# Where the query norms are applied in a local attention: from the vectors to the scale of the exponentials

## The chip, the cores and the metric

The kernel runs on one core of a Trainium2 chip. The metric is device time in microseconds (us) of one execution, as the median of several. A core has a matrix engine (PE), a vector engine (DVE), an activation engine (ACT), a general engine (POOL) and DMA queues. They run side by side and meet only at semaphores. SBUF is the memory that all of them use, PSUM the one that PE writes. "Granted clock" is the share of PE's full speed that the chip allowed in a stretch.

## The reference

Two layers, each an attention and a feed-forward block, on 8 x 128 tokens of width 128. The change touches only the last block, a local transformer of depth 2. Its attention, cut to what matters (8 heads of 64, window 64, 8 tiles of 128 tokens per depth):

```python
q = l2norm(q) * qs
k = l2norm(k) * ksc
q, k = rotary_xpos(q, k)
bq = q.reshape(b, h, w, WINDOW, d) * QK_SCALE
sim = jnp.einsum('bhwid,bhwjd->bhwij', bq, bk)
sim = jnp.where(mask, -jnp.finfo(sim.dtype).max, sim)
attn = jax.nn.softmax(sim, axis=-1)
out = jnp.einsum('bhwij,bhwjd->bhwid', attn, bv)
```

`l2norm(t)` divides each head's vector by its length. A row of `sim` belongs to one query, so the inverse length of that query is one factor for the whole row.

## The kernel before, in words

The program is written by hand, one instruction list for each engine, with counting semaphores between them. Nothing reorders it. On DVE and ACT a `step(...)` marks an instruction as counted, and `settle()` waits until all counted instructions of the own engine have ended.

The local attention takes 2 x 8 = 16 **local tiles** i = 0 to 15 (128 tokens, all 8 heads). For tile i:

- PE `qkv(i)` projects queries and keys (1024 columns) and values (512) into PSUM banks 0 to 2. ACT `square(i)` (L1493) squares queries and keys and signals `squared`.
- DVE `rotate(i)` (L1190, L1192, L1194) waits for `squared`, multiplies by the rotary tables into R and T2; POOL adds T2 to R (L1724). DVE `sum_squares(i)` gives 16 sums per token (8 query heads, 8 key heads), ACT `head_root(i)` a first inverse root.
- DVE `unit_norm(i)` refines the 16 inverse lengths in three small steps (`newton`, L875, L877, L879) into `lr` and multiplies all 1024 columns of R by them (L1209). It signals `rope`.
- PE `turn_qk(i)` (L582) turns R, ACT `take_turned_qk(i)` (L1516, L1517) copies the result out. PE `score_band(i)` writes the band mask (`BANDED` outside the window) and `score_heads(i)` adds the scores (both L252) in banks 3 and 4.
- DVE `largest(i)` (L1216) takes the negated maximum of every row and head into `lneg` and signals `lmax`.
- ACT `exponential_half(i, c)` (L1525) has one ACTIVATE for each of 4 heads: `exp(score + bias)`, bias a column of `lneg`, and an accumulator read for the row sum. It signals `lexp`. Both halves are 8 ACTIVATEs of 128x128.
- DVE `normalise_p(i, c)` (L1229, L1232) divides by the sums, PE `turn_p`, ACT `take_turned_p` (L1538), PE `weigh`, ACT `take_turned_o` (L1510), PE `project_o`, DVE `add_output` (L1224) finish the tile.

The tiles are pipelined: while tile i is in its exponentials, tile i+1 is normalised and tile i+2 projected and rotated. In tiles 0 to 3 ACT runs `exponential(i)`, then `square(i+2)`. From tile 4 on, the feed-forward block goes along in quarters and tiles alternate:

- an **even tile** has the first half of its exponentials, then `square(i+2)`, then the second half, then the copy L1555 (Identity with a scale and a bias from SBUF), later `take_gelu` (L1565);
- an **odd tile** has all eight exponentials, and only then `square(i+2)`.

DVE's order in an even tile from 4 on is: `largest(i)`, `unit_norm(i+1)`, `quarter_rows`, `rotate(i+2)`, `sum_squares(i+2)`, `add_output(i-1)`, both `normalise_p(i)`, three `gate_third`. In an odd tile: `largest(i)`, `unit_norm(i+1)`, both `normalise_p(i)`, `add_down` (L1252), `rotate(i+2)`, moments, `sum_squares(i+2)`, `add_output(i-1)`.

Of the kernel before, what the change touches and what calls it, by code (L numbers as in the profile page):

```python
# [18 lines left out]
ALU = mybir.AluOpType  # L19
ACT = mybir.ActivationFunctionType  # L20
AX = mybir.AxisListType

P = 128
# [4 lines left out]
LH, LD = 8, 64  # L28
# [7 lines left out]
HD = 6  # L36
EPS = 1e-5
MASKED = -float(2 ** 66)
BANDED = -float(2 ** 100)
QMAX = 127.0  # L40
SOFT = 1.0 / float(np.sqrt(np.float32(D)))

# [28 lines left out]
def constants():  # L71
# [4 lines left out]
    i, j = np.arange(P)[:, None], np.arange(P)[None]  # L76
    c[:, C_BAND:C_BAND + P] = np.where((i < j) | (i > j + 64), BANDED, 0.0)
    c[:, C_ROWMASK:C_ROWMASK + HG] = (np.arange(P)[:, None] % 64) // D == np.arange(HG)[None]
# [14 lines left out]
def build(nc, x_d, ctxT_d, maskT_d, const_d, l0_d, ffn0_d, l1_d, f_d, out_d):  # L93
    with ExitStack() as stack:
        def sb(name, shape, dt=F32):
            return stack.enter_context(nc.sbuf_tensor(name, [P, *shape], dt))
# [3 lines left out]
        def sem(name):  # L100
            if name not in sems:
                sems[name] = stack.enter_context(nc.semaphore(name))
            return sems[name]
# [67 lines left out]
        lneg = sb("lneg", [2, LH])  # L171
        tabs = sb("tabs", [2, 2, 2, LD])
        ss = sb("ss", [2 * LH])
        ss_floor = sb("ss_floor", [2 * LH, 2])
        lss = sb("lss", [2 * LH])
        lr0 = sb("lr0", [2 * LH])
        lnt = sb("lnt", [2, 2 * LH])
        lr = sb("lr", [2 * LH])
        lsum = sb("lsum", [2, LH])
        lrec = sb("lrec", [LH])  # L180

# [1 line left out]
        def view(base, at, *shape):  # L183
            size = int(np.prod(shape))
            names = "abcd"[:len(shape)]
            v = base[:, at:at + size]
            return v if len(shape) == 1 else v.rearrange(f"p ({' '.join(names)}) -> p {' '.join(names)}",
                                                         **dict(zip(names, shape)))
# [3 lines left out]
        ps = stack.enter_context(nc.psum_tensor("ps", [P, 8, 512], F32))  # L192
# [20 lines left out]
        R = view(blkf, 0, 2, T)  # L213
# [619 lines left out]
        def _(dve):  # L833
            v = nc.vector
            done = [0]

            def step(i):

                i.then_inc(sem("dve_steps"), 1)
                done[0] += 1  # L840

            def settle():

                dve.wait_ge(sem("dve_steps"), done[0])
# [28 lines left out]
            def newton(x, r, tmp, out):  # L873

                step(v.tensor_tensor(tmp[:, 0, :], r, r, ALU.mult))  # L875
                settle()
                step(v.scalar_tensor_tensor(tmp[:, 1, :], tmp[:, 0, :], -0.5, x, ALU.mult, ALU.mult))  # L877
                settle()
                step(v.scalar_tensor_tensor(out, tmp[:, 1, :], 1.5, r, ALU.add, ALU.mult))  # L879
                settle()  # L880
# [229 lines left out]
            for u in range(6):  # L1110
                c, t, r = u // 3, u % 3, FT0[u % 3]
                h = HID0[0:r, t, 512 * c:512 * (c + 1)]
# [91 lines left out]
            def unit_norm(i):  # L1204
                dve.wait_ge(sem("root"), i + 1)
                dve.wait_ge(sem("pair_sum"), i + 1)
                newton(ss[:, :], lr0[:, :], lnt, lr[:, :])
                r = R[:, i % 2, :].rearrange("p (h j) -> p h j", j=LD)
                v.tensor_tensor(r, r, lr[:, :].rearrange("p (h o) -> p h o", o=1).to_broadcast([P, 2 * LH, LD]),  # L1209
                                ALU.mult).then_inc(sem("rope"), 1)  # L1210

            def largest(i):
                dve.wait_ge(sem("lscores"), i + 1)
                if i >= 2:
                    dve.wait_ge(sem("lexp"), 2 * (i - 1))
                v.tensor_reduce(lneg[:, i % 2, :], ps[:, 3:5, :].rearrange("p b (h k) -> p (b h) k", k=P),  # L1216
                                AX.X, ALU.max, negate=True).then_inc(sem("lmax"), 1)

            def add_output(i):
                n = i % NB  # L1220
# [42 lines left out]
            sum_squares(0)  # L1263
            divide_batch(4)
            unit_norm(0)
            divide_batch(5)
            rotate(1)
            sum_squares(1)
            largest(0)
            divide_batch(6)  # L1270
            unit_norm(1)
            for i in range(4):
                if i >= 1:
                    largest(i)
                if i == 0:
                    divide_batch(7)
                if i >= 1:
                    unit_norm(i + 1)
                if i == 1:
                    normalise(6, X, Z, "z_in", 4, NB)  # L1280
                normalise_p(i, 0)
                normalise_p(i, 1)
                rotate(i + 2)
                sum_squares(i + 2)
                if i == 0:
                    add_projection(1, 1)
                    moments(6, X, 4, NB)
                if i >= 1:
                    add_output(i - 1)
                if i == 3:  # L1290
                    quarter_moments(0)
            for i in range(4, 2 * NB, 2):
                largest(i)
                unit_norm(i + 1)
                quarter_rows((i - 4) // 2)
                if i + 2 < 2 * NB:
                    rotate(i + 2)
                    sum_squares(i + 2)
                add_output(i - 1)
                normalise_p(i, 0)  # L1300
                normalise_p(i, 1)
                if i + 2 == 2 * NB:
                    break

                i, q = i + 1, (i - 4) // 2
                for t in range(3):
                    gate_third(q, t)
                largest(i)
                unit_norm(i + 1)
                normalise_p(i, 0)  # L1310
                normalise_p(i, 1)
                add_down(q)
                rotate(i + 2)
                quarter_moments(q + 1)
                sum_squares(i + 2)
                add_output(i - 1)
# [18 lines left out]
        def _(act):  # L1335
# [3 lines left out]
            def step(i):  # L1339
                i.then_inc(sem("act_steps"), 1)  # L1340
                done[0] += 1

            def settle():
                act.wait_ge(sem("act_steps"), done[0])
# [30 lines left out]
            def take_output(k, c):  # L1375
# [15 lines left out]
              bias=w_x[:, A_BQK + 2:A_BQK + 3]).then_inc(sem("proj"), 1)  # L1391
# [3 lines left out]
              bias=w_x[:, A_BQK:A_BQK + 1]).then_inc(sem("proj"), 1)  # L1395
# [22 lines left out]
            for i in range(G * NCH + 2):  # L1418
# [10 lines left out]
                if i >= 2:  # L1429
                    c, q = i - 2, (i - 2) % NCH * QC  # L1430
# [24 lines left out]
            for u in range(6):  # L1455
                t, r = u % 3, FT0[u % 3]
# [62 lines left out]
            def exponential_half(i, c):  # L1519
                act.wait_ge(sem("lmax"), i + 1)  # L1520
                if i >= 2:
                    act.wait_ge(sem("pT_ps"), 2 * (i - 1))
                for j in range(4):
                    k = 4 * c + j
                    e = a(S1[:, i % 2, P * k:P * (k + 1)], ps[:, 3 + c, P * j:P * (j + 1)], ACT.Exp,  # L1525
                          bias=lneg[:, i % 2, k:k + 1], accum_out=lsum[:, i % 2, k:k + 1])
                e.then_inc(sem("lexp"), 1)

            def exponential(i):
                exponential_half(i, 0)  # L1530
                exponential_half(i, 1)
# [94 lines left out]
            for i in range(4, 2 * NB, 2):  # L1626
                q, more = (i - 4) // 2, i + 2 < 2 * NB
                take_turned_o(i - 1)
                exponential_half(i, 0)
                if more:  # L1630
                    square(i + 2)
# [13 lines left out]
                i = i + 1  # L1645
# [130 lines left out]
```

## Time and profile before

| | us |
|---|---|
| median of 3 runs | 408.64 |
| lowest, highest | 405.45, 411.32 |
| span of the profiled execution, first to last instruction | 406.5 |
| busy: PE, DVE, ACT, POOL | 352.7, 338.9, 295.9, 58.6 |

The profile has no other time of the profiled execution than its span. The span stands against the median only roughly: it lies 2.1 us below it and inside the spread of the runs. The local tiles fill the stretch from about 205 us to 388 us. Busy time says how long an engine worked, not whether somebody waited for it.

### The profile page before, as it was taken

The numbers are of one execution on the slowest core, as the hardware profiler recorded it, in microseconds if no ns is written. First come the engines' busy times: TensorE is split into PE (matmuls) and PEld (weight loads), VectorE is DVE, ScalarE is ACT, GpSimd is POOL, SyncE is SP. The second block draws the span as 40 slices with busy tenths as digits, with TensorE's granted clock in tenths as the row PEclk, the third lists the DMA queues.
The fourth block names the chain that finished last, engine by engine and source line by source line (L and its number), as shares of the span: only waits on it lengthen the run. The fifth ranks groups of instructions, "written<-read, shape, count | busy, mean of one in ns | idle before, by whom it ended". The sixth has DMA issues, their size and how long they took to land.

```text
span 406.5 us, 10233 instructions
## 1 busy us (share of the span) xinstructions
PE 352.7 (87%) x4033; PEld 251.1 (62%) x4036; DVE 338.9 (83%) x725; ACT 295.9 (73%) x727; POOL 58.6 (14%) x45
## 2 busy tenths in 40 slices
PE   2899999999945878998798889999999999998676
PEld 1498888887731424555455556567676767676565
DVE  5989987887789889979679999989899999986343
ACT  1789999896434337776747787898989898986663
POOL 2000002000003021000023123403132323212110
PEclk9999999999985699999989999999999999999779
DMA  8800010000000000000000000000000000000001
GB/s 315 347 4 3 4 42 3 3 4 3 2 0 0 2 1 0 2 2 2 0 2 2 0 0 2 0 2 2 1 2 2 1 2 0 2 2 0 2 1 52
DMA packets 1774, 8.29 MB, mean 20 GB/s; under 512 B 192, under 2 KB 448, under 8 KB 1472
## 3 DMA queue, kind: packets, MB, share of 16 engines
q1 hardware_dynamic: 1728, 7.65, 4.8%
q8 instruction: 32, 0.52, 0.6%
q14 instruction: 14, 0.11, 0.1%
HBM read 7.12 MB, written 0.52 MB: 19 GB/s over the span
## 4 chain that ended last, share of the span: by engine, by line
PE 43%; DVE 29%; ACT 17%; issue 10%; DMA 1%; DVEq 0%; ACTq 0%
PE ps L252 15%; ACT PT L1525 5%; ACT blk L1411 3%; DVE PT L1232 3%; PE ps L506 3%; DVE lneg L1216 3%; PE ps L620 3%; DVE blk L1190 2%; DVE ss_floor L1200 2%; PE ps L656 2%; ACT PT L1595 2%; PE ps L379 2%; PE ps L493 2%; DVE Y L870 2%; PE ps L582 2%
## 5 line engine op out<-in xcount | busy, mean ns | idle before, releaser
L1724 POOL TENSOR_TENSOR blk<-blk 128x1024 f32<-128x1024 f32 x16 | 37.7, 2359 | 170.6 <-DVE blk L1194 170.6
L568 PE MATMUL ps<-w_f,full 128*128 128x512 f32 x96 | 48.2, 619 | 0.9 <-issue 0.9
L1525 ACT ACTIVATE PT<-ps,lneg 128x128 f32<-128x128 f32 x128 | 45.0, 377 | 5.3 <-DVE lneg L1216 5.3
L252 PEld LDWEIGHTS ps<-blk,st 128*128 128x128 bf16 x768 | 26.8, 98 | 3.8
L1045 DVE TENSOR_REDUCE mneg<-ps 128x4 bf16<-128x512 bf16 x32 | 22.0, 688 | 7.7 <-PE ps L357 7.4
L1525 ACT ACTIVATION_READ_ACCUMULATOR PT<-ps,lneg 128x1 f32 x128 | 27.9, 218 | 0.0
L252 PE MATMUL ps<-blk,rel 128*128 128x64 bf16 x768 | 27.6, 193 | 0.0
L252 PE MATMUL ps<-blk,st 128*128 128x64 bf16 x768 | 27.6, 193 | 0.0
L1582 ACT ACTIVATE PT<-ps 128x512 f32<-128x512 f32 x32 | 17.5, 595 | 13.2 <-PE ps L506 13.2
L1216 DVE TENSOR_REDUCE lneg<-ps 128x8 f32<-128x1024 f32 x16 | 19.6, 1223 | 8.6 <-PE ps L252 8.5
L1232 DVE TENSOR_TENSOR PT<-PT,lrec 128x512 f32<-128x512 f32 x32 | 25.3, 790 | 1.1
L568 PEld LDWEIGHTS ps<-w_f,full 128*128 128x128 f32 x96 | 16.3, 192 | 13.7 <-issue 13.6
L252 PEld LDWEIGHTS ps<-blk,rel 128*128 128x128 bf16 x768 | 24.6, 98 | 0.0
L1426 ACT ACTIVATE St<-ps 128x512 bf16<-128x512 f32 x32 | 19.3, 604 | 7.0 <-PE ps L252 6.9
L620 PE MATMUL ps<-const,PT 128*128 128x128 f32 x128 | 19.3, 288 | 5.5 <-ACT blk L1517 2.9
L506 PEld LDWEIGHTS ps<-const,PT 128*128 128x128 f32 x128 | 14.1, 143 | 15.1 <-ACT PT L1595 13.8
L1411 ACT ACTIVATE blk<-blk,const 128x128 bf16<-128x128 bf16 x32 | 23.3, 984 | 0.0
L656 PE MATMUL ps<-YT,w_f 128*128 128x256 f32 (+1 forms) x96 | 22.5, 384 | 0.6 <-DVE blk L1194 0.3
L1190 DVE TENSOR_TENSOR blk<-ps,tabs 128x1024 f32<-128x1024 f32 x16 | 19.5, 1218 | 3.8 <-ACT blk L1493 3.8
L1538 ACT ACTIVATE PT<-ps 128x512 f32<-128x512 f32 x32 | 17.5, 602 | 5.6 <-PE ps L620 5.6
L620 PEld LDWEIGHTS ps<-const,PT 128*128 128x128 f32 x128 | 14.5, 145 | 10.3 <-ACT blk L1517 3.7
L506 PE MATMUL ps<-const,PT 128*128 128x128 f32 x128 | 17.9, 284 | 3.1 <-ACT PT L1595 2.8
(234 smaller groups left out, 905.5 us busy)
## 6 DMA issues: line engine op xcount, KB each, us to landing
w_f<-f_dram SPq DMA_DIRECT2D x2, 1689.0 KB, 13.3
w_x<-l_dram SPq DMA_DIRECT2D x1, 774.0 KB, 5.9
w_f<-ffn_dram SPq DMA_DIRECT2D x1, 561.0 KB, 7.9
X<-x_dram SPq DMA_DIRECT2D x1, 512.0 KB, 3.6
ctxT<-ctxT_dram SPq DMA_DIRECT2D x1, 512.0 KB, 4.4
OT<-maskT_dram SPq DMA_DIRECT2D x1, 512.0 KB, 7.1
rest<-l_dram SPq DMA_DIRECT2D x1, 385.0 KB, 4.8
const<-const_dram SPq DMA_DIRECT2D x1, 324.0 KB, 6.3
```

What stands on the lines that cost most here:

```text
L252: return mm(out, l, r, start=start, stop=False, skip_group_check=True)
L506: i = tr(ps[:, 4 + c, P * j:P * (j + 1)], S1[:, u % 2, P * (4 * c + j):P * (4 * c + j + 1)], ident)
L568: m = mm(ps[:, c, :], hT[:, n, :], w_f[:, l, F_QKV + 512 * c:F_QKV + 512 * (c + 1)], start=True, stop=True)
L620: t = tr(ps[:, 5 + c, P * j:P * (j + 1)], S1[:, i % 2, P * (4 * c + j):P * (4 * c + j + 1)], ident)
L656: x = mm(ps[0:r, first + t, 256 * m:256 * (m + 1)], w_f[:, l, F_W1 + HID * m + P * t:F_W1 + HID * m + P * t + r], YT[:, 256 * j:256 * (j + ...
L1045: v.tensor_reduce(mneg[:, c % 2, :], turned_b[:, c % 2, :].rearrange("p (j k) -> p j k", j=4), AX.X, ALU.max).then_inc(sem("chunk_max"), 1)
L1190: step(v.tensor_tensor(heads(R[:, i % 2, :]), u, tab[:, 0].to_broadcast([P, 2, LH, LD]), ALU.mult))
L1216: v.tensor_reduce(lneg[:, i % 2, :], ps[:, 3:5, :].rearrange("p b (h k) -> p (b h) k", k=P), AX.X, ALU.max, negate=True).then_inc(sem("lma ...
L1232: v.tensor_tensor(p, p, r.rearrange("p (h o) -> p h o", o=1).to_broadcast([P, 4, P]), ALU.mult)\
L1411: i = a(ring[:, c % RING, :, :, :, h].rearrange("p b n q -> p (b n) q"), src, ACT.Copy, scale=const[:, C_ROWMASK + h:C_ROWMASK + h + 1])
L1525: e = a(S1[:, i % 2, P * k:P * (k + 1)], ps[:, 3 + c, P * j:P * (j + 1)], ACT.Exp, bias=lneg[:, i % 2, k:k + 1], accum_out=lsum[:, i % 2, ...
L1724: g_.tensor_tensor(R[:, i % 2, :], R[:, i % 2, :], T2, ALU.add).then_inc(sem("pair_sum"), 1)
```

## The change

The queries stay unnormalised. Their inverse lengths come in later: once in the maximum (`lbias` = `lneg` times the inverse length, a small new instruction on DVE behind the maximum), and once as the per-token scale of the exponential, which becomes `exp(scale * score + bias)` with both operands from SBUF. L1209 covers the 512 columns of the keys alone. `lr` gets two buffers, since it is now read by ACT later on. `BANDED` is smaller, so that its product with an inverse length stays finite.

```diff
-BANDED = -float(2 ** 100)
+BANDED = -float(2 ** 80)
...
-        lr = sb("lr", [2 * LH])
+        lr = sb("lr", [2, 2 * LH])
+        lbias = sb("lbias", [2, LH])
...
-                newton(ss[:, :], lr0[:, :], lnt, lr[:, :])
-                r = R[:, i % 2, :].rearrange("p (h j) -> p h j", j=LD)
-                v.tensor_tensor(r, r, lr[:, :].rearrange("p (h o) -> p h o", o=1).to_broadcast([P, 2 * LH, LD]),
+                rate = lr[:, i % 2, :]
+                newton(ss[:, :], lr0[:, :], lnt, rate)
+                r = R[:, i % 2, 512:1024].rearrange("p (h j) -> p h j", j=LD)
+                v.tensor_tensor(r, r, rate[:, LH:2 * LH].rearrange("p (h o) -> p h o", o=1).to_broadcast([P, LH, LD]),
                                 ALU.mult).then_inc(sem("rope"), 1)
...
-                v.tensor_reduce(lneg[:, i % 2, :], ps[:, 3:5, :].rearrange("p b (h k) -> p (b h) k", k=P),
-                                AX.X, ALU.max, negate=True).then_inc(sem("lmax"), 1)
+                step(v.tensor_reduce(lneg[:, i % 2, :], ps[:, 3:5, :].rearrange("p b (h k) -> p (b h) k", k=P),
+                                     AX.X, ALU.max, negate=True))
+                settle()
+                v.tensor_tensor(lbias[:, i % 2, :].rearrange("p (c j) -> p c j", c=2),
+                                lneg[:, i % 2, :].rearrange("p (c j) -> p c j", c=2),
+                                lr[:, i % 2, 0:LH].rearrange("p (j c) -> p c j", c=2), ALU.mult).then_inc(sem("lmax"), 1)
...
                     e = a(S1[:, i % 2, P * k:P * (k + 1)], ps[:, 3 + c, P * j:P * (j + 1)], ACT.Exp,
-                          bias=lneg[:, i % 2, k:k + 1], accum_out=lsum[:, i % 2, k:k + 1])
+                          scale=lr[:, i % 2, 2 * j + c:2 * j + c + 1], bias=lbias[:, i % 2, k:k + 1], accum_out=lsum[:, i % 2, k:k + 1])
```

DVE in an even tile i from 4 on, from the maximum of tile i to the rotation of tile i+2, as it was:

```order
L1216 TENSOR_REDUCE lneg<-ps 128x8
L875 TENSOR_TENSOR lnt<-lr 128x16
L877 SCALAR_TENSOR_TENSOR lnt<-lnt,ss 128x16
L879 SCALAR_TENSOR_TENSOR lr<-lnt,lr 128x16
L1209 TENSOR_TENSOR blk<-blk,lr 128x1024
L875 TENSOR_TENSOR nt<-r 128x2
L877 SCALAR_TENSOR_TENSOR nt<-nt,ve 128x2
L879 SCALAR_TENSOR_TENSOR rstd<-nt,r 128x2
L870 TENSOR_SCALAR Y<-O,mv,rstd 128x128 x2
L1190 TENSOR_TENSOR blk<-ps,tabs 128x1024
```

And as it is now (`blk` is R, line numbers are 1 to 6 higher):

```order
L1218 TENSOR_REDUCE lneg<-ps 128x8
L1221 TENSOR_TENSOR lbias<-lneg,lr 128x8
L876 TENSOR_TENSOR lnt<-lr 128x16
L878 SCALAR_TENSOR_TENSOR lnt<-lnt,ss 128x16
L880 SCALAR_TENSOR_TENSOR lr<-lnt,lr 128x16
L1211 TENSOR_TENSOR blk<-blk,lr 128x512
L876 TENSOR_TENSOR nt<-r 128x2
L878 SCALAR_TENSOR_TENSOR nt<-nt,ve 128x2
L880 SCALAR_TENSOR_TENSOR rstd<-nt,r 128x2
L871 TENSOR_SCALAR Y<-O,mv,rstd 128x128 x2
L1191 TENSOR_TENSOR blk<-ps,tabs 128x1024
```

One instruction is added between the maximum and its signal, and the multiplication is half as wide. On ACT nothing changes place; the exponentials of the same even tile and what follows them now read:

```order
L1516 ACTIVATE full<-ps 128x512
L1531 ACTIVATE PT,lsum<-ps,lbias,lr 128x128 x4
L1499 ACTIVATE blk<-ps 128x1024
L1531 ACTIVATE PT,lsum<-ps,lbias,lr 128x128 x4
L1561 ACTIVATE YT<-ps,w_f 128x256
```

Each of the 8 exponentials of a tile names two SBUF operands (`lbias`, `lr`) where it named one (`lneg`).

## Rows read from the trace of the kernel before

**Rows 1.** The page: span, and busy time of each engine.
```profile
span 406.5 us, 10233 instructions
...
PE 352.7 (87%) x4033; PEld 251.1 (62%) x4036; DVE 338.9 (83%) x725; ACT 295.9 (73%) x727; POOL 58.6 (14%) x45
```

**Rows 2.** Chain of waits (start us, us, what) in odd tile 7.
```profile
292.51 1.18 ACT PT L1525 x6
```

**Rows 3.** Timeline of DVE (start us, us), tiles 7 and 8.
```profile
293.72 0.18 DVE L1229 RECIPROCAL lrec<-lsum 128x4 f32<-128x4 f32 x1 [0.40 <-ACT PT L1525]
...
299.86 1.22 DVE L1216 TENSOR_REDUCE lneg<-ps 128x8 f32<-128x1024 f32 x1 [0.16 <-PE ps L252]
301.00 0.17 DVE L875 TENSOR_TENSOR lnt<-lr 128x16 f32<-128x16 f32 x1
301.20 0.17 DVE L877 SCALAR_TENSOR_TENSOR lnt<-lnt,ss 128x16 f32<-128x16 f32 x1
...
301.62 1.23 DVE L1209 TENSOR_TENSOR blk<-blk,lr 128x1024 f32<-128x1024 f32 x1
...
303.87 1.22 DVE L1190 TENSOR_TENSOR blk<-ps,tabs 128x1024 f32<-128x1024 f32 x1
...
309.38 0.69 DVE L1232 TENSOR_TENSOR PT<-PT,lrec 128x512 f32<-128x512 f32 x1
```

**Rows 4.** Timeline of ACT, the same two tiles.
```profile
290.79 0.37 ACT L1525 ACTIVATE PT<-ps,lneg 128x128 f32<-128x128 f32 x1 [0.30 <-DVE lneg L1216]
...
293.54 1.06 ACT L1493 ACTIVATE blk<-ps 128x1024 f32<-128x1024 f32 x1
...
300.89 0.60 ACT L1510 ACTIVATE full<-ps 128x512 f32<-128x512 f32 x1 [0.80 <-PE ps L628]
301.38 0.36 ACT L1525 ACTIVATE PT<-ps,lneg 128x128 f32<-128x128 f32 x1
...
301.72 0.37 ACT L1525 ACTIVATE PT<-ps,lneg 128x128 f32<-128x128 f32 x1
...
302.79 1.02 ACT L1493 ACTIVATE blk<-ps 128x1024 f32<-128x1024 f32 x1
...
305.08 0.59 ACT L1555 ACTIVATE YT<-ps,w_f 128x256 f32<-128x256 f32 x1
305.53 0.62 ACT L1499 ACTIVATE blk<-ps 128x512 f32<-128x512 f32 x1
...
309.43 1.19 ACT L1565 ACTIVATE PT<-ps,w_f 128x256 f32<-128x256 f32 x3
```

**Rows 5.** Groups by line and shape, ACT, whole span (busy us, mean ns).
```profile
L1538 ACT ACTIVATE PT<-ps 128x512 f32<-128x512 f32 x32 | 17.5, 602 | 5.6 <-PE ps L620 5.6
...
L1565 ACT ACTIVATE PT<-ps,w_f 128x256 f32<-128x256 f32 x16 | 6.8, 470 | 0.6 <-PE ps L656 0.4
...
L1555 ACT ACTIVATE YT<-ps,w_f 128x256 f32<-128x256 f32 x8 | 4.6, 581 | 1.3 <-PE ps L649 1.3
...
L1460 ACT ACTIVATE PT<-ps,gusc 128x512 f32<-128x512 f32 x4 | 2.7, 687 | 2.7 <-PE ps L454 2.6
```

**Rows 6.** Timelines of ACT and DVE: squares and rotations behind tiles 0 and 1.
```profile
218.89 1.07 ACT L1493 ACTIVATE blk<-ps 128x1024 f32<-128x1024 f32 x1
...
230.19 1.06 ACT L1493 ACTIVATE blk<-ps 128x1024 f32<-128x1024 f32 x1
...
220.40 1.22 DVE L1190 TENSOR_TENSOR blk<-ps,tabs 128x1024 f32<-128x1024 f32 x1
...
232.32 1.22 DVE L1190 TENSOR_TENSOR blk<-ps,tabs 128x1024 f32<-128x1024 f32 x1
```

**Rows 7.** Windows: us, busy us (instructions) of each engine, granted clock, DMA.
```profile
289.50:299.90 10.40, 10.19 (x82) 7.73 (x84) 9.54 (x22) 9.50 (x32) 2.53 (x2) 1.00 0.01 2
...
366.90:377.40 10.50, 8.51 (x74) 7.10 (x76) 5.77 (x15) 6.38 (x24) 1.33 (x3) 1.00 0.00 0
...
382.10:388.40 6.30, 5.34 (x32) 4.30 (x30) 2.94 (x13) 2.39 (x7) 1.57 (x2) 0.55 0.02 4
```

## The prediction

> **What bounds the kernel now.** I read the page's busy times first, then windows of one tile each, then the chain of waits through two tiles, and last the timelines of DVE and ACT beside each other. By busy time PE and DVE lead and ACT trails [rows 1], which would favour a change that takes work off DVE. The window of an odd tile says less: in 10.40 us PE is busy 10.19, DVE 9.54, ACT 9.50 [rows 7]. All three are nearly full, so what counts is who waits last, and that differs between even and odd tiles.
>
> In an **odd tile** the chain runs through ACT: maximum, all eight exponentials [rows 2], then the second row sums, for which DVE sat idle 0.40 us [rows 3], then DVE and PE to the scores of the next tile. The square for the rotation also stands behind the eight exponentials [rows 4]. Whatever DVE saves between the maximum and those row sums only lengthens its idle time.
>
> In an **even tile** the chain is shown on DVE: maximum, newton, L1209, the rows of the feed-forward, rotation. But the rotation starts at 303.87 [rows 3] and needs the square, which ends at 302.79 + 1.02 = 303.81 [rows 4]. Between the two lie 0.06 us, of which I count 0.03 as slack and 0.03 as the release. So ACT is a second chain of the same length: the copy L1510 at 300.89, four exponentials from 301.38, the square at 302.79. Behind the rotation DVE is in one piece up to the row sums, and PE waits for it.
>
> **The change part by part.**
>
> *L1209 at half width.* 128x1024 takes 1.23 us; 128x512 of the same operation with the same kinds of operands takes 0.69 (L1232) [rows 3]. Saved: 0.54 us of DVE in each of 16 tiles.
>
> *The new `lbias`.* An instruction of this size is L875 with 0.17 us, and one that waits for it starts 0.20 after its start [rows 3]. It must wait for the end of the maximum: 1.22 us and 0.03 to release, where L875 now starts 1.14 behind the maximum's start [rows 3]. So DVE loses 0.11 for the wait and some 0.10 for the instruction, whose end overlaps L875: 0.21 us. DVE's net is -0.33 us a tile. The signal `lmax` comes 0.20 us later. Queued behind the wait is newton for the next tile, which nobody needs at once; waiting for `lmax` is ACT. In odd tiles ACT was idle 0.30 us at that point [rows 4], so it starts 0.20 later. In even tiles ACT is held by L1510: the first exponential starts at 301.38, and the later `lmax` comes at 299.86 + 1.22 + 0.03 + 0.20 = 301.31, which costs nothing.
>
> *The second operand from SBUF.* This is the term that decides, and no row shows such an exponential. With no such operand a 128x512 activation takes 602 ns, with a scale from SBUF (L1460) 687: +85. A 128x256 one with a bias takes 470 (L1565), with scale and bias 581 (L1555): +111 [rows 5]. From start to start, which is what a queue pays, L1565 needs (1.19 - 0.47) / 2 = 0.36 us and L1555 305.53 - 305.08 = 0.45 [rows 4]: +0.09. These rows bound it at 0.085 and 0.111; below them stands nothing at all, if the accumulator read behind each exponential hides it. I take 0.09, because L1555 also stands in the queue directly behind an exponential's accumulator read. The pitch of an exponential is 301.72 - 301.38 = 0.34 [rows 4] and becomes 0.43: +0.72 us for eight, +0.36 for four. The Trainium skill ("ScalarE: Activation LUTs", section "What ACT_TABLE_LOAD costs") speaks against the change in the same way: it gives about 93 ns for each per-partition pointer operand. By it the eight would cost 0.74; no run here shows it for an exponential with accumulator.
>
> *Wider effects.* `lr`'s second buffer and `BANDED` cost nothing: no instruction changes shape. POOL, PE and the DMA queues issue the same instructions in the same order. `rope` comes earlier, but PE turns tile i+1 only behind work that waits for the exponentials.
>
> *Odd tiles.* DVE's 0.33 us fall into its idle time before the second row sums. The chain grows by 0.20 + 0.72 = 0.92 us. The square ends 0.92 later too, with the row sums and the rotation. Tiles 5, 7, 9, 11, 13, 15: 5.5 us. In tile 15 the end of the kernel hangs on the same eight exponentials.
>
> *Even tiles.* The square ends 0.36 later, 0.03 of it is slack: the rotation starts 0.33 us later, although DVE would be ready 0.33 earlier. Six tiles, 4 to 14 (14 has no rotation, but the copy L1555 behind its exponentials feeds PE; I give it the same): 2.0 us. The second half's 0.36 goes into the row sums four microseconds later and is hidden by the rotation; if that cover went, it would cost 0.36 more a tile.
>
> *Tiles 0 to 3* have all exponentials ahead of the square. Tile 0: the square ends at 218.89 + 1.07 = 219.96, DVE rotates at 220.40 [rows 6], so 0.44 - 0.03 of 0.92 are covered: +0.51. Tile 1: the square ends at 230.19 + 1.06 = 231.25, moved by 0.51 + 0.92 to 232.68, the rotation from 232.32 [rows 6] to 232.71: the running sum falls from 0.51 to 0.39. Tiles 2 and 3 have the idle time of odd tiles: +0.92 each. Together 2.2 us.
>
> **Sum:** 2.2 + 2.0 + 5.5 = +9.7 us, or 406.5 [rows 1] to 416.2 of the profiled execution. Its span is 2.1 us below the median of the runs; on 408.64 the forecast is 418.3, +2.4%. With 0.085 and 0.111 in place of 0.09 the some 104 exponentials on the path (ten tiles with eight, six with four) give -0.5 and +2.2: +9.2 to +11.9.
>
> **The rivals.**
>
> *The second operand is free* (15%). For it speaks that the accumulator read could cover a fetch; against it, that an accumulator read also precedes L1555, and L1555 pays. Then odd tiles pay 0.20 for `lmax` (six, and two of the first four), even tiles gain 0.03, tiles 0 and 1 gain 0.2 to 0.3 each: 1.6 - 0.2 - 0.5 = +0.9 us, 409.5. Same within 2%.
>
> *DVE is the bound after all* (5%), as the chain shows it in even tiles. Then every tile gains 0.33: 16 x 0.33 = 5.3 us, 403.3, not slower. It needs a free second operand and a square that ends 0.33 us before DVE comes, where the rows leave 0.06; it decides from the point where the four exponentials get shorter, not longer. The Trainium skill ("VectorE: DVE Perf Modes", section "The DRAIN you can't avoid") says that the next DVE operation starts only when the pipe is empty and that a semaphore between two costs nothing extra. By it `settle()` would be free and the gain 16 x 0.44 = 7.0 us, 401.6. The trace disagrees: L875 starts 0.08 us before the maximum ends [rows 3].
>
> *PE's clock falls* (8%). PE gets longer pauses, and in the window 382.10 to 388.40, which follows tile 15's pauses, the clock is 0.55 [rows 7]. If it fell like that for half of PE's 10.19 us in an odd tile [rows 7], that half would take twice as long, 5.1 us more; in five tiles 25 us, 444. Against it: PE was busy 8.51 of 10.50 us, 81%, at full clock [rows 7], and an odd tile will still have 10.19 in 11.3, 90%.
>
> *The forecast* has the remaining 72%.
>
> **How the numbers follow.** A change of under 2% (8.2 us) can't be told from none on this kernel. The forecast's +9.2 to +11.9 lies above it, but the smallest values near it, and the runs before spread by 5.9 us: of its 72% I count 60 as slower by over 2%, 12 as within. With the clock 68% slower; within 2% 12 + 15 + 3 = 30%, rounded down to 29; faster by over 2%, from the DVE case alone, 2%, to which I add 1. The forecast's own range is 408.64 + 9.2 to + 11.9 with 2 us of run scatter on both sides: 415.8 to 422.5. To leave out no more than 20%, the range reaches down to the free operand, with its scatter cut: 410 to 423.
>
> **What would show it.** The mean of L1525 rises from about 377 to about 465 ns and its pitch from 0.34 to 0.43. L1209 shows 0.69. `lbias` shows 0.17, and L875 starts 1.35 us behind the maximum's start in place of 1.14. DVE's idle time in odd tiles grows from 0.40 to about 1.7 us before the two row sums. In even tiles DVE shows a new wait of about 0.6 us ahead of L1190, released by the square. A pair of tiles takes 23.6 us where 22.4 stood. The forecast is wrong if the pitch stays at 0.34, if the wait ahead of L1190 doesn't appear, or if the granted clock leaves 1.00 between 215 and 385 us.

## The result, and the profile after

| | before | after |
|---|---|---|
| median, us | 409.92 (4 runs) | 417.37 (4 runs) |
| lowest, highest | 405.45, 411.32 | 416.41, 417.50 |
| ratio | | 1.0217, 95% interval 1.0171 to 1.0263 |
| span of the profiled execution | 406.5 | 415.6 |

The change is slower by some 2%: the ratio says 2.2%, and the spans +9.1 us where +9.7 was forecast. The two medians differ by less, 7.45 us or 1.8%: the forecast stood on 408.64, the median of three runs before, and a fourth of 411.21 moved it to 409.92. The interval of the ratio reaches below 2%; a second set of rounds of the same kernel gave 1.0207 (1.0171 to 1.0244). So it is slower beyond doubt, and by over 2% most likely, not surely.

The page after, answering to [rows 1] (span; busy time by engine) and to the group of the exponentials:

```profile
span 415.6 us, 10249 instructions
...
PE 351.0 (84%) x4033; PEld 249.7 (60%) x4036; DVE 334.6 (81%) x741; ACT 307.5 (74%) x727; POOL 58.6 (14%) x45
...
L1531 ACT ACTIVATE PT<-ps,lbias,lr 128x128 f32<-128x128 f32 x128 | 56.8, 466 | 6.6 <-DVE lbias L1221 6.6
```

Before, the exponentials read:

```profile
L1525 ACT ACTIVATE PT<-ps,lneg 128x128 f32<-128x128 f32 x128 | 45.0, 377 | 5.3 <-DVE lneg L1216 5.3
```

DVE is busy 4.3 us less than before, as wanted, and ACT 11.6 more: 128 exponentials at 466 ns where they took 377. The span grew all the same.

Timeline of DVE after, the same two tiles (7 and 8) as [rows 3]:

```profile
293.46 1.23 DVE L1218 TENSOR_REDUCE lneg<-ps 128x8 f32<-128x1024 f32 x1 [0.67 <-PE ps L253]
294.72 0.17 DVE L1221 TENSOR_TENSOR lbias<-lneg,lr 128x8 f32<-128x8 f32 x1
294.81 0.17 DVE L876 TENSOR_TENSOR lnt<-lr 128x16 f32<-128x16 f32 x1
...
295.43 0.69 DVE L1211 TENSOR_TENSOR blk<-blk,lr 128x512 f32<-128x512 f32 x1
296.83 0.18 DVE L1235 RECIPROCAL lrec<-lsum 128x4 f32<-128x4 f32 x1 [0.70 <-ACT PT L1531]
...
298.59 0.18 DVE L1235 RECIPROCAL lrec<-lsum 128x4 f32<-128x4 f32 x1 [0.86 <-ACT PT L1531]
...
304.74 1.23 DVE L1218 TENSOR_REDUCE lneg<-ps 128x8 f32<-128x1024 f32 x1 [0.17 <-PE ps L253]
...
309.07 1.23 DVE L1191 TENSOR_TENSOR blk<-ps,tabs 128x1024 f32<-128x1024 f32 x1 [0.57 <-ACT blk L1499]
```

L1211 shows the 0.69 of the narrow multiplication. In the odd tile DVE then waits 0.70 and 0.86 us for row sums, where it had waited 0.40 once: 1.56 us, with "about 1.7" forecast. In the even tile a wait of 0.57 us for the square stands ahead of the rotation, where none was.

Timeline of ACT after, answering to [rows 4]:

```profile
294.92 0.46 ACT L1531 ACTIVATE PT<-ps,lbias,lr 128x128 f32<-128x128 f32 x1 [0.48 <-DVE lbias L1221]
295.28 0.19 ACT L1531 ACTIVATION_READ_ACCUMULATOR PT<-ps,lbias,lr 128x1 f32 x1
295.37 0.45 ACT L1531 ACTIVATE PT<-ps,lbias,lr 128x128 f32<-128x128 f32 x1
...
306.25 0.45 ACT L1531 ACTIVATE PT<-ps,lbias,lr 128x128 f32<-128x128 f32 x1
...
306.69 0.46 ACT L1531 ACTIVATE PT<-ps,lbias,lr 128x128 f32<-128x128 f32 x1
...
308.00 1.04 ACT L1499 ACTIVATE blk<-ps 128x1024 f32<-128x1024 f32 x1
```

The pitch is 306.69 - 306.25 = 0.44 us, 0.34 before. The square starts 1.75 behind the first exponential, 1.41 before.

### The profile page after: what moved, and what is told of

The parts are those of the page before. It is cut to its first block, busy times and chain, and to the rows that moved or that the text cites. A ratio compares the mean times of both kernels' runs of the same rounds, so it can differ in the third digit from the quotient of the medians.

```text
span 415.6 us, 10249 instructions
## 1 busy us (share of the span) xinstructions
PE 351.0 (84%) x4033; PEld 249.7 (60%) x4036; DVE 334.6 (81%) x741; ACT 307.5 (74%) x727; POOL 58.6 (14%) x45
## 4 chain that ended last, share of the span: by engine, by line
PE 43%; DVE 24%; ACT 23%; issue 7%; DMA 1%; SPq 0%; DVEq 0%; ACTq 0%
PE ps L253 15%; ACT PT L1531 10%; ACT blk L1417 3%; DVE lneg L1218 3%; PE ps L507 3%; DVE PT L1238 3%; PE ps L621 3%; DVE blk L1191 2%; DVE ss_floor L1201 2%; ACT blk L1499 2%; PE ps L629 2%; ACT PT L1601 2%; PE ps L265 2%; PE ps L494 2%; PE ps L380 2%
## 5 line engine op out<-in xcount | busy, mean ns | idle before, releaser
L1531 ACT ACTIVATE PT<-ps,lbias,lr 128x128 f32<-128x128 f32 x128 | 56.8, 466 | 6.6 <-DVE lbias L1221 6.6
L569 PE MATMUL ps<-w_f,full 128*128 128x512 f32 x96 | 47.3, 609 | 0.9 <-issue 0.9
L1531 ACT ACTIVATION_READ_ACCUMULATOR PT<-ps,lbias,lr 128x1 f32 x128 | 27.3, 213 | 0.0
L621 PE MATMUL ps<-const,PT 128*128 128x128 f32 x128 | 18.7, 282 | 8.1 <-ACT blk L1523 5.7
L1161 DVE TENSOR_REDUCE m<-ps 128x8 f32<-128x1024 f32 x16 | 19.5, 1219 | 1.4 <-PE ps L494 1.4
```

Source lines behind the costliest of these rows:

```text
L569: m = mm(ps[:, c, :], hT[:, n, :], w_f[:, l, F_QKV + 512 * c:F_QKV + 512 * (c + 1)], start=True, stop=True)
L621: t = tr(ps[:, 5 + c, P * j:P * (j + 1)], S1[:, i % 2, P * (4 * c + j):P * (4 * c + j + 1)], ident)
```

## The experiments

**How they are read.** The runs of the kernel before spread from 405.3 to 411.3 us, and spans of one program differ too: `no_max` below was profiled twice, with 396.9 and 394.6 us. In these two all of it lies ahead of the local tiles: rotation 1 starts at 211.41 and at 208.99 us. Two stretches there differ in granted clock. Windows of the first profile, then of the second (us, busy us (instructions) of PE, weight load, DVE, ACT, POOL, then clock, DMA):

```profile
130.00:140.00 10.00, 7.08 (x29) 3.37 (x29) 8.13 (x19) 4.95 (x7) 0.00 (x0) 0.54 0.00 0
...
200.00:212.00 12.00, 10.16 (x81) 5.55 (x80) 6.99 (x14) 7.11 (x13) 2.35 (x1) 0.86 0.00 1
```
```profile
130.00:140.00 10.00, 7.08 (x41) 3.62 (x41) 8.77 (x20) 4.95 (x7) 0.00 (x0) 0.63 0.00 0
...
200.00:212.00 12.00, 10.10 (x92) 5.87 (x93) 9.41 (x17) 7.71 (x15) 2.89 (x2) 1.00 0.01 2
```

I therefore also compare the **stage** from the start of rotation 1 to that of rotation 15, by the first instruction of `rotate` in the timelines of DVE. Its two ends, before and then after:

```profile
211.03 1.22 DVE L1190 TENSOR_TENSOR blk<-ps,tabs 128x1024 f32<-128x1024 f32 x1
...
362.06 1.21 DVE L1190 TENSOR_TENSOR blk<-ps,tabs 128x1024 f32<-128x1024 f32 x1
```
```profile
211.10 1.22 DVE L1191 TENSOR_TENSOR blk<-ps,tabs 128x1024 f32<-128x1024 f32 x1
...
370.74 1.22 DVE L1191 TENSOR_TENSOR blk<-ps,tabs 128x1024 f32<-128x1024 f32 x1
```

In all of these kernels the granted clock of the stage is 1.00. Its length repeats: 159.64 and 159.52 us in two profiles of the changed kernel, 145.49 in both of `no_max`. The **odd step** is the time from rotation 8 to 9, with the eight exponentials of odd tile 7 in it, the **even step** that from 9 to 10, with the first four of even tile 8. Tiles 14 and 15 lie behind the stage.

| kernel | ratio to before, 95% | stage, us | odd step | even step |
|---|---|---|---|---|
| before | | 151.03 | 13.42 | 8.99 |
| `pointer_only` | 1.0170 (1.0111 to 1.0229) | 157.91 | 14.15 | 9.32 |
| `bias_only` | 1.0058 (1.0019 to 1.0096) | 153.80 | 13.61 | 9.19 |
| `keys_only` | 0.9939 (0.9908 to 0.9970) | 149.84 | 13.43 | 8.97 |
| `one_operand` | 1.0027 (0.9989 to 1.0064) | 151.76 | 13.62 | 8.97 |
| the change | 1.0217 (1.0171 to 1.0263) | 159.64 | 14.34 | 9.33 |
| `after_again` | 1.0207 (1.0171 to 1.0244) | 159.52 | 14.33 | 9.31 |
| `no_max` | 0.9755 (0.9716 to 0.9794) | 145.49 | 12.74 | 9.25 |
| `no_max_scale` | 0.9799 (0.9760 to 0.9837) | 146.93 | 13.13 | 8.97 |
| `no_max_keys` | 0.9644 (0.9594 to 0.9695) | 143.91 | 12.74 | 9.26 |

### The second operand alone

```diff
-                          bias=lneg[:, i % 2, k:k + 1], accum_out=lsum[:, i % 2, k:k + 1])
+                          scale=ones[:, 2 * j + c:2 * j + c + 1], bias=lneg[:, i % 2, k:k + 1], accum_out=lsum[:, i % 2, k:k + 1])
```

`ones` is a new tile, filled with 1.0 at the start.

> The kernel before, with one thing added: each local exponential takes a scale of 1.0 from SBUF beside its bias. Nothing else moves; the result is the same. Theory (the second operand is the cost, and ACT is on the path): pitch 0.34 to 0.44 us, odd tiles +0.72 us, even tiles +0.33, tile 0 +0.3, tile 1 nothing, tiles 2 and 3 +0.72: about +8.0 us, 1.95 % slower than before. Rival (the operand is free): +0 us. Rival (DVE is the bound): ACT's extra time hides, under +2 us.

Measured: +6.9 us in the stage, ratio 1.0170 (1.95% expected, inside the interval), and +7.5 us from rotation 1 to the end (about +8.0 expected). The exponential of this kernel:

```profile
L1527 ACT ACTIVATE PT<-ps,lneg,ones 128x128 f32<-128x128 f32 x128 | 56.8, 467 | 4.8 <-DVE lneg L1218 4.8
```

467 ns, as in the change. The odd step grows by 0.73 us (0.72 expected), the even one by 0.33 (0.33 expected). The free operand is refuted, and so is an ACT whose extra time hides: this is four fifths of the change's 8.6 us in the stage. Behind rotation 15 another thing comes in: from 377 to 382 us the granted clock was 0.75, in the stretch in which PE turns tile 15 (L583, eight matmuls in 1.92 us against 1.04 in the changed kernel at full clock). From rotation 15 to the second row sums of tile 15 this kernel needs 22.42 us, the changed one 21.30. PE had paused 0.70 and 1.29 us just before, in the changed kernel 0.70 and 0.84. So a fall of the clock behind PE's pauses did happen in one of these kernels, outside the stage; why here and not in the change is open.

### The small instruction alone

```diff
+                settle()
+                v.tensor_tensor(lbias[:, i % 2, :].rearrange("p (c j) -> p c j", c=2),
+                                lneg[:, i % 2, :].rearrange("p (c j) -> p c j", c=2),
+                                ones[:, 0:LH].rearrange("p (j c) -> p c j", c=2), ALU.mult).then_inc(sem("lmax"), 1)
...
-                          bias=lneg[:, i % 2, k:k + 1], accum_out=lsum[:, i % 2, k:k + 1])
+                          bias=lbias[:, i % 2, k:k + 1], accum_out=lsum[:, i % 2, k:k + 1])
```

> The kernel before, with the small instruction alone: the maximum is awaited and multiplied by ones into lbias, which the exponentials take as bias; queries are normalised as before, exponentials keep one SBUF operand. Theory: lmax 0.20 us later in odd tiles and tiles 2 and 3 (8 x 0.20), and DVE 0.21 longer in even tiles and tiles 0 and 1, where nothing is saved on L1209 to pay for it (8 x 0.2): +3.2 us. Rival (waiting on the own engine costs nothing, only the instruction's 0.1 us counts on DVE): +2.4 us. Rival (ACT alone bounds): +1.6 us.

Measured: +2.8 us in the stage, some 0.20 in each of its 14 tiles (3.2 for 16, as expected); by the ratio 0.8 to 3.9 us. Its profiled span is 406.5, that of before to the digit, since its rotation 1 starts 2.1 us earlier (208.91 against 211.03) and what follows rotation 15 takes 0.65 less, at a clock of 0.92 against 0.87. The steps grow by 0.19 and 0.20. Timeline of DVE in this kernel, an even tile:

```profile
299.30 1.23 DVE L1219 TENSOR_REDUCE lneg<-ps 128x8 f32<-128x1024 f32 x1 [0.17 <-PE ps L254]
300.56 0.17 DVE L1222 TENSOR_TENSOR lbias<-lneg,ones 128x8 f32<-128x8 f32 x1
300.64 0.17 DVE L877 TENSOR_TENSOR lnt<-lr 128x16 f32<-128x16 f32 x1
```

L877 starts 1.34 us behind the maximum's start; before it was 1.14 (299.86 to 301.00 in [rows 3]). Of the 0.20, the wait for the maximum's end takes 0.12 (1.26 against 1.14) and the instruction 0.08. A semaphore on the own engine is thus not free here.

### The narrow multiplication alone

```diff
-                r = R[:, i % 2, :].rearrange("p (h j) -> p h j", j=LD)
-                v.tensor_tensor(r, r, lr[:, :].rearrange("p (h o) -> p h o", o=1).to_broadcast([P, 2 * LH, LD]),
+                r = R[:, i % 2, 512:1024].rearrange("p (h j) -> p h j", j=LD)
+                v.tensor_tensor(r, r, lr[:, LH:2 * LH].rearrange("p (h o) -> p h o", o=1).to_broadcast([P, LH, LD]),
```

> The kernel before, with L1209 on the 512 key columns alone; the queries' inverse lengths are left out of the computation altogether. It is the change's saving without its costs: 0.54 us of DVE in 16 tiles, 8.6 us. Theory: odd tiles and tiles 2, 3 nothing (DVE idles there for the row sums), even tiles 0.03, tiles 0 and 1 0.4 and 0.5: about -1 us, not to be told from before. Rival (DVE is the bound): -5 to -8.6 us.

Measured: -1.2 us in the stage, ratio 0.9939, which its interval does tell from before. The ratio says 2.5 us: the span has another 1.3 behind rotation 15, and 0.9 of that lies behind the second row sums of tile 15, where the clock was 0.85 against 0.78. The odd and the even step change by +0.01 and -0.02 us; most of the gain lies in the first tiles: rotation 3 starts 20.36 us behind rotation 1, 21.29 before. 8.6 us less work (16 x 0.54; busy time fell by 7.5) on an engine with 83% busy time bring 1.2 us.

### The change without its second operand

```diff
-                          scale=lr[:, i % 2, 2 * j + c:2 * j + c + 1], bias=lbias[:, i % 2, k:k + 1], accum_out=lsum[:, i % 2, k:k + 1])
+                          bias=lneg[:, i % 2, k:k + 1], accum_out=lsum[:, i % 2, k:k + 1])
```

> The changed kernel, with the exponentials back to one SBUF operand (bias from lneg, scale 1.0 in the instruction); lbias is still computed and lmax still signalled behind it. The queries' inverse lengths are thereby left out of the softmax. Theory: the operand's +9 us vanish, what stays is lbias against the narrower L1209: +0.9 us over before (8 x 0.20, less 0.2 in even tiles, less 0.5 in tiles 0 and 1). Rival (the cost lies in lbias and its wait): still +5 us or more.

Measured: +0.7 us in the stage, ratio 1.0027, the same as before. The odd step keeps the 0.20 of the later signal, the even one has nothing. Everything else of the slowdown, 159.64 - 151.76 = 7.9 us of the stage, is the scale from SBUF. Alone, in `pointer_only`, it cost 6.9. Most of the 1.0 between lies in tiles 0, 1 and 4: there it costs 0.73, 0.23 and 0.37 on top of this kernel and only 0.32, 0.02 and 0.09 on top of before, where ACT still had slack.

### The change once more

> The changed kernel once more, word for word, for a narrower interval. Theory: +9.1 us by the profile's spans, ratio 1.022 with both ends above 1.017. Rival (part of the difference was the spread of the runs before): 1.015 or less.

Measured: 1.0207, both ends above 1.017, and the stage 0.12 us from the first profile's. The span was 416.7 against 415.6; the two differ behind the second row sums of tile 15, where the clock was 0.78 here and 0.86 in the first profile (next section).

### Without the maximum

The maximum protects the exponential from overflow. With unit queries and keys, learned scales of one and keys no later than the query, a score is at most 8, and it can go. This holds for these inputs and for moderate learned scales, not in general.

```diff
-            def largest(i):
-                dve.wait_ge(sem("lscores"), i + 1)
...
-                act.wait_ge(sem("lmax"), i + 1)
+                act.wait_ge(sem("lscores"), i + 1)
...
-                          bias=lneg[:, i % 2, k:k + 1], accum_out=lsum[:, i % 2, k:k + 1])
+                          accum_out=lsum[:, i % 2, k:k + 1])
```

> The kernel before without the maximum: no L1216, exponentials with no SBUF operand at all, released by the scores. With unit queries and keys and a causal window of 64 a score is at most 8 times the products of the learned scales (here ones), so exp needs no shift. Theory (the exponentials' chain bounds odd tiles, the square bounds even ones): odd tiles lose 1.26 + 0.72 us until PE binds, even tiles 0.36, tiles 0 to 3 1.2 to 2 each: -14 to -18 us. Rival (DVE is the bound, 16 x 1.14): -18 us. Rival (PE is the next bound at once): -5 us or less.

Measured: ratio 0.9755, span 396.9 (-9.6), stage -5.5 us. It is the fastest version here that computes the reference, but the forecast of -14 to -18 was wrong, and by more than the span says: up to the second row sums of tile 15 the kernel gains 7.9 us (5.5 in the stage and 2.4 behind it), and 2.1 more come from there to the end, where the same work ran at a clock of 0.89 against 0.78. The chain of waits of this kernel, from the row sums of even tile 6 to the rotation in even tile 8 (start us, us, what):

```profile
283.62 0.70 DVE PT L1225
284.32 0.04 issue
284.36 0.66 PE ps L620 x4
285.02 1.09 PE ps L252 x16
286.11 1.02 PE ps L628 x16
287.13 1.92 PE ps L568 x4
289.05 1.34 PE ps L698 x12
290.39 0.86 PE ps L568 x2
...
297.08 1.93 PE ps L568 x4
299.01 0.02 issue
299.03 1.03 ACT blk L1480
300.06 0.02 issue
300.09 1.22 DVE blk L1190
```

From 284.36 to 299.01 the chain never leaves PE. Then it goes through the square, the rotation and DVE's row sums back to PE: a loop of 22.0 us for two tiles, against 22.4 before. I had priced only what left the old chain, and had called PE's next place a rival of "-5 us or less".

### The change without the maximum

```diff
-                          scale=lr[:, i % 2, 2 * j + c:2 * j + c + 1], bias=lbias[:, i % 2, k:k + 1], accum_out=lsum[:, i % 2, k:k + 1])
+                          scale=lr[:, i % 2, 2 * j + c:2 * j + c + 1], accum_out=lsum[:, i % 2, k:k + 1])
```

`largest`, with `lbias`, and its signal are gone as above.

> The changed kernel without the maximum and without lbias: exponentials take the queries' inverse lengths as scale, one SBUF operand, no bias. DVE has 0.54 us a tile less to do than in the variant that normalises the queries and drops the maximum, ACT 0.09 us more for each of 8 exponentials. Theory (operands on ACT count, width on DVE doesn't): odd tiles -1.26, even tiles 0, tiles 0 to 3 1.2 each: -12 us against before, 3 to 6 us slower than the variant with full-width normalisation. Rival (DVE is the bound): 5 to 8 us faster than that variant.

Measured: 0.9799, stage +1.4 us over `no_max`, medians 400.95 and 398.95. The sign is as expected, the size is below the 3 to 6 us. With PE next in line only 0.1 us of a pair (22.1 against 22.0) is left of the operand's price. This comparison also holds a narrower L1209; `no_max_keys` below has it narrow too, and against that one the operand costs 3.0 us of the stage (146.93 against 143.91). Exponentials with no SBUF operand (`no_max`), then with the scale alone:

```profile
L1512 ACT ACTIVATE PT<-ps 128x128 f32<-128x128 f32 x128 | 33.3, 290 | 0.5 <-PE ps L252 0.5
```
```profile
L1514 ACT ACTIVATE PT<-ps,lr 128x128 f32<-128x128 f32 x128 | 45.0, 377 | 0.5 <-PE ps L253 0.5
```

### Why no more came of it

The edit is the narrow L1209 of `keys_only` put on `no_max`, and `scale=0.125`, an immediate.

> The variant without the maximum, with L1209 on the 512 key columns alone and an immediate scale of 0.125 in the exponentials; the queries' inverse lengths are left out of the computation. It takes 0.54 us of DVE from each tile and adds no SBUF operand. It tells why the maximum's removal gave 9.6 us of span and not 14 to 18. Theory (PE has become the bound of both kinds of tile there): 0 to -1 us against the variant without the maximum, pair of tiles 22.0 us as before. Rival (DVE is still the bound there): -4 us or more. And the 2 us by which the variant with the scale in the exponentials was slower are then the operand's alone.

> The variant without the maximum once more, beside the one with narrow L1209, for the difference of the two: ratio to before 0.975 again, span within 1 us of 396.9.

Measured: 395.43 against 397.80 us, spans 393.5 and 394.6. A pair of tiles takes 22.0 us in both (12.74 + 9.26, 12.74 + 9.25): DVE isn't the bound there, which refutes the rival for the tiles from 4 on. The stage is 1.6 us shorter all the same, all of it between rotations 2 and 6 (34.13 against 35.75 us); so "0 to -1" was short. By the medians the gain is 2.4 us; of it, as far as the two profiles show, 1.1 lies behind the second row sums of tile 15, at a clock of 1.00 against 0.90. The exponentials with the immediate scale take 290 ns, as with none: what costs is the operand from SBUF. `no_max_again` gave 0.9726 (0.9674 to 0.9779) and a span of 394.6, 2.3 us below the first, with a stage equal to 0.01 us. That is more than the 1 us I had expected. It lies ahead of rotation 1, where the two stretches shown above differ in clock.

## Why the prediction was right

**The second operand** was put at +0.09 us of pitch from start to start, +0.72 and +0.36 in eight and four. Measured on the same tiles: 0.44 for 0.34. Duration 466 for 377, +89 ns; the three levels 290, 377 and 466 make each operand 87 to 89 ns. The figure of the Trainium skill ("ScalarE: Activation LUTs", section "What ACT_TABLE_LOAD costs"), about 93 ns for each pointer operand, lies a little above it. The accumulator read behind each exponential hid nothing of it: duration and pitch grew alike. The rows that bounded the term, at 85 and 111 ns, belong to other functions and widths; that the middle was right was a good guess, which `pointer_only` confirmed.

**Odd tiles:** +0.92 forecast, 14.34 - 13.42 = +0.92 measured, and the two experiments give its parts, 0.73 and 0.19. **Even tiles:** +0.33 forecast, 9.33 - 8.99 = +0.34 measured. The wait ahead of the rotation is 0.57 us ("about 0.6"). That `lbias` costs nothing in even tiles is shown by `one_operand` (-0.02).

**Tiles 0 to 3:** forecast 0.51, -0.12, 0.92, 0.92. The rotations start at 211.10, 221.00, 232.82, 242.78 and 252.69 us after, against 211.03, 220.40, 232.32, 241.29 and 250.31: +0.53, -0.10, +0.99, +0.89.

**DVE's saving** was said to fall into idle time; `keys_only` shows it, with -1.2 us for 8.6.

**The sum.** The stage has +8.6. Behind it the scores of tile 15 come 15.69 us after the rotation, 15.35 before: +0.34; the second row sums 5.61 behind the maximum's start, 4.68 before: +0.93. Ahead of the stage 0.07. That makes +9.95 where 9.7 was said. The one step that I hadn't is behind tile 15: windows of before and after, and of the changed kernel's other profile, from the second row sums to the end:

```profile
382.09:406.50 24.41, 18.15 (x104) 15.50 (x102) 10.38 (x36) 11.85 (x25) 2.93 (x4) 0.78 0.06 22
```
```profile
392.04:415.60 23.56, 17.17 (x102) 14.29 (x102) 10.38 (x36) 11.86 (x25) 2.94 (x4) 0.86 0.07 23
```
```profile
392.02:416.70 24.68, 18.36 (x102) 15.68 (x102) 10.38 (x36) 11.85 (x25) 2.93 (x4) 0.78 0.06 22
```

The same work, 24.41, 23.56 and 24.68 us, at clocks of 0.78, 0.86 and 0.78. The other kernels agree: the stretch takes 23.49 at 0.86 in `bias_only`, 22.66 at 0.89 in `pointer_only` and 21.38 at 1.00 in `no_max_keys`. So the -0.85 that brings +9.95 to +9.1 belongs to that profile's clock and not to the change. By the other profile, at the clock of before, the span grew by 10.2. That the forecast was met within 0.6 us is thus not as sharp as it looks: the clock outside the stage moves a span by more. The same holds for 418.3 against 417.37, since the median before moved by 1.3 us.

**The rivals.** A free operand is refuted by `pointer_only`, DVE as the bound by `keys_only`. The clock stayed at full speed in the stage although PE now pauses 1.10 us in each odd tile; in `pointer_only`, behind the stage, it did not. PE's pause, and the window of tile 7 after:

```profile
299.88 0.44 PE L553 MATMUL ps<-const,zv 128*128 128x128 f32 x2 [1.10 <-DVE zv L1258]
```
```profile
293.46:304.74 11.28, 10.13 (x82) 7.68 (x84) 9.24 (x23) 10.21 (x31) 2.51 (x2) 1.00 0.01 2
```

The window says what the page of the profile doesn't: ACT, 74% busy over the span, is busy 10.21 of 11.28 us here.

The wait on the own engine was priced rightly at 0.11 us; `bias_only` shows 0.12. The Trainium skill ("VectorE: DVE Perf Modes", section "The DRAIN you can't avoid") was cited for a free wait, with one half of what it says. It reports that a semaphore behind each operation cost nothing extra in a series of eight copies. But the section also says that "A next op that is not held starts earlier". The second is what this trace shows: L875 started 0.08 us before the maximum's end, and a wait takes that head start away.

## What to carry to other kernels

A factor that is folded into an activation as a scale from SBUF isn't free: here each such operand costs some 0.09 us an instruction, so eight 128-column exponentials paid 0.72 us to save one 0.54 us piece of vector work. Before moving work from the engine with more busy time, look in one period of the trace at who waits for whom; the saving fell into a wait and the cost onto the chain. And when an edit takes a piece out of the chain, price what the next chain allows, as the variant without the maximum shows: 2.3 us (1.98 and 0.36) were to leave a pair of tiles, and 0.4 came of it (22.41 to 21.99).

## What the runs showed that I hadn't expected

- The local stage repeats to 0.1 us between profiles of one kernel (159.64 and 159.52; 145.49 twice), while spans of the same kernels differ by 1.1 and 2.3 us. The difference lies where the clock changes: ahead of the stage (0.54 or 0.63, 0.86 or 1.00) for `no_max`, and behind tile 15 (0.78 or 0.86) for the change. For 1 us effects the stage tells more than the runs.
- The even step got longer without the maximum (9.25 against 8.99): the square there waits for PE, whose queue is full through the odd tile before.
